# Attention and FFN block on one core: queries and keys in two float32r parts of 48 rows, batches in alternating partition halves, and a slot's exponent banks ahead of its maximum banks

## What is computed

```python
xn = layernorm(x)                                   # x: 8 batches x 512 tokens x 256
Q, K, V = xn @ W_q.T, xn @ W_k.T, xn @ W_v.T        # 16 heads of 16 values
Qr, Kr = rope(Q), rope(K)
scores = einsum('bhqd,bhkd->bhqk', Qr, Kr) * 16 ** -0.5   # causal mask
attn = softmax(scores) @ V, heads joined, @ W_o.T
ffn = fake_fp8(xn) @ fake_fp8(weight).T + bias      # one scale for each tensor
out = x + attn + ffn
```

## Time and profile before

| | |
|---|---|
| median of 3 runs | 481.37 us (481.06 to 482.79) |
| the profiled execution's span | 479.7 us |
| PE busy | 413.3 us, 86% |
| DVE busy | 352.8 us, 74% |
| ACT, POOL busy | 278.5 us, 274.8 us |
| DMA moved | 57.55 MB, mean 120 GB/s |

### The profile page before, as it was taken

One profiled execution on the slowest core, in us unless ns is written; L12 is line 12 of the kernel. 1 busy time (PEld: TensorE's weight loads), 2 busy tenths in 40 slices (PEclk: granted clock), 3 DMA queues, 4 the chain that ended last, 5 costly groups with the idle time before them and its releaser, 6 DMA issues.

```text
span 479.7 us, 10238 instructions
## 1 busy us (share of the span) xinstructions
PE 413.3 (86%) x2819; PEld 224.7 (47%) x2819; DVE 352.8 (74%) x1340; ACT 278.5 (58%) x500; POOL 274.8 (57%) x278
## 2 busy tenths in 40 slices
PE   1771667899999999999999969999999999998976
PEld 1431411264346455645564535545555544554544
DVE  3779799868779887988798827978897868852041
ACT  2734731047765776577657742587468665666840
POOL 2204576436747963796389631985498427327560
PEclk9995555599999999999999986999999999999997
DMA  7728458211482339323923391145714671020021
GB/s 249 254 76 223 107 178 198 66 46 44 153 202 93 100 104 199 135 86 117 243 92 108 109 227 48 44 135 152 189 56 135 165 196 39 5 86 6 1 87 45
DMA packets 39789, 57.55 MB, mean 120 GB/s; under 512 B 5280, under 2 KB 31264, under 8 KB 39712
## 3 DMA queue, kind: packets, MB, share of 16 engines
q1 hardware_dynamic: 39744, 57.03, 42.0%
HBM read 35.78 MB, written 17.04 MB: 110 GB/s over the span
## 4 chain that ended last, share of the span: by engine, by line
PE 44%; POOL 18%; DMA 11%; issue 11%; ACT 7%; DVE 4%; SPq 3%; ACTq 0%; POOLq 0%; DVEq 0%
PE o_ps L935 9%; PE st_ps L854 9%; DMA qk_parts<-parts 8%; PE s_ps L871 7%; PE m_ps L907 5%; PE m_ps L810 4%; POOL parts L268 4%; PE m_ps L882 4%; ACT prob L734 3%; POOL prob L440 3%; POOL rot L264 3%; POOL rot L258 2%; POOL xq L470 2%; SPq L370 2%; POOL qv L466 2%
## 5 line engine op out<-in xcount | busy, mean ns | idle before, releaser
L599 DVE CUSTOM_DVE_ANT_0 scratch<-s_ps,causal 128x512 bf16<-128x512 f32 (+3 forms) x512 | 224.2, 487 | 64.4 <-PE s_ps L871 53.7
L734 ACT ACTIVATE prob<-st_ps 128x512 f32<-128x512 f32 x320 | 175.6, 600 | 104.4 <-PE st_ps L854 104.2
L440 POOL TENSOR_SCALAR_AFFINE_SELECT prob<-prob 128x512 f32<-128x512 f32 (+1 forms) x160 | 86.8, 546 | 141.8 <-ACT prob L734 141.0
L871 PE MATMUL s_ps<-k_st,q_st 96*128 96x512 bf16 (+3 forms) x512 | 132.4, 322 | 21.8 <-DVE rowmax L599 18.6
L854 PE MATMUL st_ps<-q_st,k_st 98*128 98x128 bf16 (+3 forms) x512 | 121.1, 303 | 1.0 <-ACT prob L734 0.9
L935 PE MATMUL o_ps<-prob,v_sb 128*17 128x512 f32 (+3 forms) x1024 | 87.8, 439 | 6.0 <-ACT heads L749 5.2
L871 PEld LDWEIGHTS s_ps<-k_st,q_st 96*128 96x128 bf16 x512 | 47.1, 99 | 73.3 <-DVE rowmax L599 48.2
L854 PEld LDWEIGHTS st_ps<-q_st,k_st 98*128 98x128 bf16 x512 | 43.5, 98 | 64.5 <-ACT prob L734 26.8
L599 DVE DVE_READ_ACCUMULATOR2_ANT rowmax<- 128x1 f32 x512 | 42.3, 83 | 0.0
L935 PEld LDWEIGHTS o_ps<-prob,v_sb 128*17 128x17 f32 x1024 | 20.4, 96 | 44.1 <-issue 35.6
L907 PE MATMUL m_ps<-wo_sb,attnT 128*128 128x256 f32 x128 | 35.1, 398 | 1.0 <-ACT attnT L755 0.5
(11 more groups left out here) (96 smaller groups left out, 496.7 us busy)
## 6 DMA issues: line engine op xcount, KB each, us to landing
qk_parts<-parts SPq DMA_DIRECT2D x16, 768.0 KB, 3.8
q_st<-qk_parts SPq DMA_DIRECT2D x32, 192.0 KB, 3.6
k_st<-qk_parts SPq DMA_DIRECT2D x32, 192.0 KB, 3.7
q_st<-x_dram SPq DMA_DIRECT2D x8, 512.0 KB, 5.4
q_st<-qk_parts SPq DMA_DIRECT2D x32, 128.0 KB, 3.7
k_st<-qk_parts SPq DMA_DIRECT2D x32, 128.0 KB, 3.7
xn_v<-xnT SPq DMA_DIRECT2D x8, 512.0 KB, 3.7
x_res<-x_dram SPq DMA_DIRECT2D x8, 512.0 KB, 3.5
```

What stands on the lines that cost most here:

```text
L440: eng.affine_select(out=ap, in_=ap, compare_op=ALU.is_ge, fill=0.0, base=0, pattern=pat, channel_multiplier=-1).then_inc(masked, 1)
L599: eng.tensor_tensor_reduce(scratch[:, f % 2, col:col + w], s_ps[f % 2][:, col:col + w], causal[:, T - w:T], 1.0, NEG, ALU.add, ALU.max, ro ...
L734: eng.activation(prob[u][:, half * T:(half + 1) * T], st_ps[ST_BANK[2 * s + half]][:, :], ACT.Exp, scale=SCALE).then_inc(exp_done, 1)
L871: mm = eng.matmul(s_ps[f % 2][:, col:col + (qb + 1) * P], q_st[0:ROWS, 1 - par, h, qb * P:(qb + 1) * P], k_st[0:ROWS, 1 - par, h, 0:(qb + ...
```

## The change

Queries and keys are split into two float32r parts (`high`, then `low` straight from it; `remainder` and `middle` are gone). A head's stack has 48 rows (three products of 16), plus two shift rows. A batch of even number lies in partitions 0 to 49, one of odd number in 64 to 113 (`HALF * par`), so `q_st` and `k_st` hold two batches in two partition halves. In a slot the two exponent banks (`attend`) are issued first and the two maximum banks (`compare`) second. Stacks are read in two runs instead of three, 8 KB instead of 4 KB a row. The rotated values lie in the second part's place (`rotated_in`), so `rotate` waits for the store of the batch before (`parts_out`). The x batches get places of their own in eight other buffers (`x_of`), the first loops are unrolled, and the ones rows of `k_st` are written by two DMAs instead of a memset.

```diff
-Q_PARTS = ((0, 1), (0, 1, 2), (0,))
-K_PARTS = ((0, 1, 2), (0,), (0, 1))
-ROWS = 6 * DH
+Q_PARTS = ((0,), (0, 1))
+K_PARTS = ((0, 1), (0,))
+ROWS = 3 * DH
+HALF = P // 2
...
-    for n in range(4):
+    for n in range(NB):
         step(n, n % 2)
         between(n)
-    with eng.Fori(2, NB // 2) as i:
...
-        q_st = sb("q_st", [P, 2, H, T], BF16)
-        k_st = sb("k_st", [P, 2, H, T], BF16)
+        q_st = sb("q_st", [P, H, T], F32R)
+        k_st = sb("k_st", [P, H, T], F32R)
...
-        parts = sb("parts", [P, 2, 3, 2, T], BF16)
+        parts = sb("parts", [P, 2, 2, 2, T], F32R)
...
         def rotate(eng, n, w):
             eng.wait_ge(roped, 4 * n + 2 * w + 2)
             if not (isinstance(n, int) and n == 0):
-                eng.wait_ge(low_done, 2 * n + w)
+                eng.wait_ge(parts_out, 32 * (n - 1) + 16 * (w + 1))
...
-        def remainder(eng, n, w):
+        def low(eng, n, w):
             eng.wait_ge(rotated, 4 * n + 2 * w + 2)
             eng.wait_ge(hi_done, 2 * n + w + 1)
-            buf = rotated_in(n, w)
-            eng.tensor_tensor(buf, buf, parts[:, w, 0], ALU.subtract).then_inc(rem_done, 1)
-        def low(eng, n, w):
-            eng.wait_ge(mid_done, 2 * n + w + 1)
-            eng.tensor_tensor(parts[:, w, 2], rotated_in(n, w), parts[:, w, 1], ALU.subtract).then_inc(low_done, 1)
+            eng.tensor_tensor(parts[:, w, 1], rotated_in(w), parts[:, w, 0].bitcast(F32), ALU.subtract)\
+               .then_inc(low_done, 1)
...
                 for g in range(NG):
+                    if g == 0 and isinstance(n, int) and n == 0:
+                        eng.wait_ge(consts, 6)
+                        for first in (ROWS, HALF + ROWS):
+                            eng.dma_start(k_st[first:first + SHIFT, :, :].rearrange("p h (a t) -> p (h a) t", t=P).bitcast(F32),
+                                          ones2[:, None, :].to_broadcast([SHIFT, H * NQ, P])).then_inc(ones_in, 16)
                     read_stack(n, par, g, "k", busy)
...
-            eng.memset(k_st[ROWS:ROWS + SHIFT, :, :, :].rearrange("p a h t -> p (a h t)").bitcast(F32),
-                       float(np.array([0x3F803F80], np.uint32).view(np.float32)[0])).then_inc(consts, 1)
...
                     for half in range(2):
-                        i = 2 * s + half
+                        for at in range(2):
+                            if 3 in stages and at < len(unit_parts(u, half)):
+                                attend(s, half, at)
+                    for half in range(2):
+                        for at in range(2):
+                            if 2 in stages and at < len(MAX_BANKS[(2 * s + half) % len(MAX_BANKS)]):
+                                compare(2 * s + half, at)
+                def attend(s, half, at):
...
+                    h, lo = g * HG + j, HALF * par
+                    mm = eng.matmul(st_ps[ST_BANK[i]][:, col:col + T - kb * P],
+                                    k_st[lo:lo + ROWS + SHIFT, h, kb * P:(kb + 1) * P],
+                                    q_st[lo:lo + ROWS + SHIFT, h, kb * P:T], start=True, stop=True)
...
+                def compare(f, at):
...
+                    h, lo = 2 * pair + i, HALF * (1 - par)
+                    mm = eng.matmul(s_ps[f % 2][:, col:col + (qb + 1) * P],
+                                    q_st[lo:lo + ROWS, h, qb * P:(qb + 1) * P],
+                                    k_st[lo:lo + ROWS, h, 0:(qb + 1) * P], start=True, stop=True)
```

More of the change, by code:

```diff
@@ L244, in work, with rotated_in @@
             return [(s, kind, k) for s, kind, k in MISC if stage_of[ahead[kind][k]] in stages]
-        def rotated_in(n, w):
-            own = isinstance(n, int) and (n, w) == (0, 1)
-            return heads[:, 0:2, :] if own else rot[:, :, :]
+        def rotated_in(w):
+            return parts[:, w, 1].bitcast(F32)
         def rotate(eng, n, w):
@@ L366, in read_stack @@
                 src = qk_dram[par, w].rearrange("t r j h n -> (t r j) h n")
-                row = 0
+                row = HALF * par
                 for run_ in runs:
                     rows = DH * len(run_)
-                    eng.dma_start(dst[row:row + rows, par, h0:h0 + HG, :],
+                    eng.dma_start(dst[row:row + rows, h0:h0 + HG, :].bitcast(F32),
                                   src[DH * run_[0]:DH * run_[0] + rows, h0:h0 + HG, :]).then_inc(stack_in[g], 16)
@@ L405, in _ @@
                               base=0, pattern=[[-1, P]], channel_multiplier=1).then_inc(consts, 1)
+            eng.memset(v_sb[:, :, :, :], 1.0).then_inc(consts, 1)
             def invert(n, p):
@@ L456, in iteration @@
                         if s in (5, 10):
-                            remainder(eng, n, s // 10)
+                            low(eng, n, s // 10)
                     if 4 in stages:
@@ L693, in parts_of_first @@
                         high(0, w)
-                        middle(0, w)
                     high(1, 0)
@@ L846, in scores @@
                     g, u = divmod(s, 5)
-                    if u == 0 and g % 2 == 0:
+                    if 3 in stages and u == 0 and g % 2 == 0:
                         eng.wait_ge(shift_in[g // 2], 16 * (b + 1))
                     for half in range(2):
-                        i = 2 * s + half
-                        wait_past(eng, exp_done, HALVES * b + ST_BEFORE[i] + 1)
-                        for j, kb, col in unit_parts(u, half):
-                            h = g * HG + j
-                            mm = eng.matmul(st_ps[ST_BANK[i]][:, col:col + T - kb * P],
-                                            k_st[0:ROWS + SHIFT, par, h, kb * P:(kb + 1) * P],
-                                            q_st[0:ROWS + SHIFT, par, h, kb * P:T], start=True, stop=True)
+                        for at in range(2):
+                            if 3 in stages and at < len(unit_parts(u, half)):
+                                attend(s, half, at)
@@ L857, in scores @@
                         mm.then_inc(st_full, 1)
-                        if half == 0 and 2 in stages:
-                            scores_for_max(2 * s)
-                def scores_for_max(f):
+                def compare(f, at):
                     pair, m = divmod(f, len(MAX_BANKS))
-                    if f % (BANKS // NG) == 0:
+                    if at == 0 and f % (BANKS // NG) == 0:
                         g = f // (BANKS // NG)
-                        eng.wait_ge(stack_in[g], 16 * 6 * (n + 1))
-                    wait_past(eng, max_done, ITEMS * n + (ITEMS_UP_TO[f - 2] if f >= 2 else ITEMS_UP_TO[f - 2] - ITEMS))
-                    for i, qb, col in MAX_BANKS[m]:
-                        h = 2 * pair + i
-                        mm = eng.matmul(s_ps[f % 2][:, col:col + (qb + 1) * P],
-                                        q_st[0:ROWS, 1 - par, h, qb * P:(qb + 1) * P],
-                                        k_st[0:ROWS, 1 - par, h, 0:(qb + 1) * P], start=True, stop=True)
-                    mm.then_inc(s_full, 1)
+                        eng.wait_ge(stack_in[g], 16 * 4 * (n + 1))
+                    if at == 0:
+                        wait_past(eng, max_done,
+                                  ITEMS * n + (ITEMS_UP_TO[f - 2] if f >= 2 else ITEMS_UP_TO[f - 2] - ITEMS))
+                    i, qb, col = MAX_BANKS[m][at]
+                    h, lo = 2 * pair + i, HALF * (1 - par)
+                    mm = eng.matmul(s_ps[f % 2][:, col:col + (qb + 1) * P],
+                                    q_st[lo:lo + ROWS, h, qb * P:(qb + 1) * P],
+                                    k_st[lo:lo + ROWS, h, 0:(qb + 1) * P], start=True, stop=True)
+                    if at == len(MAX_BANKS[m]) - 1:
+                        mm.then_inc(s_full, 1)
@@ L966, in iteration @@
                 for s in range(SLOTS):
-                    if 3 in stages:
+                    if 2 in stages or 3 in stages:
                         scores(s)
-                    elif 2 in stages:
-                        scores_for_max(2 * s)
-                    if 2 in stages:
-                        scores_for_max(2 * s + 1)
-                        if 3 not in stages:
-                            spread_maxima(s)
+                    if 2 in stages and 3 not in stages:
+                        spread_maxima(s)
                     for at, item in enumerate(todo):
```

83 lines of the change are left out of this document (34 added, 49 removed).

## The result

The changed kernel takes 529.71 us (median of 4 runs, 523.49 to 552.47) against 482.08 us (median of 4, 481.06 to 482.83): the ratio is 1.0898, 95% interval 1.0833 to 1.0964. The prediction was 524 us in a range of 478 to 542. The profiled execution has a span of 524.7 us, 45.0 above that of before.

What follows compares the result with a forecast made beforehand. The prediction took PE's order of work to bound the main loop. It summed 479.7 + 19.5 + 41.5 - 18.2 - 2 + 1.9 = 522.4 us for the profiled execution, with the median 1.7 above: 524 us, range 478 to 542.

Steps and rivals of the forecast that it cites:

- the likeliest case: Main loop: shape changes cost and the halves overlap at slot seams; 492 to 538 us, 524 as summed, chance 0.52.
- What bounds it: Main loop: PE's order of work is the time, busy 46.0 of 47.2 us; gains on other engines count almost nothing.
- 1, float32r matmuls: Score matmuls in float32r cost more, mostly in 128-column banks: +2.6 us an iteration, +19.5 us in all.
- rival E: Short float32r score matmuls take the two float32 passes: 551 us, chance 0.03.
- 2, changes of shape: Between half-array scores and other items: 0.18 us a change into a bare load, 5.8 us an iteration, +41.5 us.
- 3, two halves at once: At slot seams, last exponent and first maximum matmuls overlap: 2.6 us an iteration, -18.2 us in all.
- Full iterations of 52 to 54 us: Main loop: the iteration length named beforehand as a sign that the forecast was right.
- the 0.09 us behind an item: Sign of a right forecast: a score matmul behind an item starts some 0.09 us late, its load starting with it.
- 4, what moves: Lighter POOL and ACT work, stores, stacks and DMAs cost 0; PE's own waits may shrink: -2 us in all.
- 5, the start: Before the main loop: -2.1 us from dropped remainders, +4 us in iteration -1 from bare loads; sum +1.9 us.
- the clock: Main loop: a clock below 1.00 was named as what would break all of the forecast; no size given.

Runs made afterwards that it cites:

- whole-array run: Changed kernel with score matmuls reading 98 and 96 rows of a constant float32r tile from iteration 0 on, in the whole-array shape: 520.79 us.
- bfloat16 run: Kernel before with its bfloat16 score matmuls cut to rows 0 to 49 and 0 to 47 of the same stacks: 508.53 us, ratio 1.0487.
- one-half run: Changed kernel with score matmuls reading 50 and 48 rows of a constant float32r tile from iteration 0 on, all in partitions 0 to 49: 593.28 us.
- 66-row run: Changed kernel with score matmuls reading 66 rows of a constant float32r tile from iteration 0 on, in the whole-array shape: 530.68 and 531.33 us.

## Why the prediction was right, and which steps were not

The total, the sign and the likeliest case were right: changes of shape cost, halves overlap, and PE's time is the kernel's. The size of several terms was not, and errors of both signs cancelled. That the total came so close is luck: without the half clock (an estimate of 19 us, below) and the start's wait (7.9 us), neither of which the sum had, the profiled execution would have taken some 498 us, not the 522.4 of the sum.

**What bounds it.** Right. In the changed kernel's full-clock iteration PE is busy 48.0 of 49.3 us, and nothing shows a gain from POOL's and ACT's lighter work (33.3 to 30.1 and 31.4 to 29.5 us), though no run has it alone. But "a gain on another engine counts almost nothing" no longer holds: six slots of an iteration wait for VectorE's `row_max`, an estimate of 3.9 us.

**1, float32r matmuls.** Nearly right. The forecast was 2.6 us plus 1.1 for the bare loads behind `pv` (counted in part 2), 3.7; the whole-array run measures +4.0. In that run a pair of 128 and 384 columns takes 0.06 + 0.23 = 0.29 us from start to start, against the 0.285 worked out from a transpose, so the half-rate rival E fell. The sum was right and its split was not: the next matmul was to stand 0.11 us behind the one of 128 columns, and it stands 0.06 behind it.

**2, changes of shape.** The mechanism is right, the price was a little high: 26 new ones at 0.18 us were 4.7, measured 3.8 (0.15 each). The bfloat16 run shows the drain by itself, 0.09 us, as forecast. Start by start, the one-half run has 4.3 us more than the whole-array run at and behind the changes, and two slots that wait for `row_max` give back 0.6 of it: most of the miss is a cost that fell into a wait. The rule of the Trainium skill that the prediction named ("TensorEngine Tiling (Array Packing)", Key Properties: a change of tiling mode drains the TensorE) agrees with these traces: 0.09 us a change.

**3, two halves at once.** This step failed, beyond its own bounds of 0 and -3.7 us an iteration: measured -5.8. The step read "the other three quarters of the scores follow one in their own half and can't". They did: TensorE started a maximum matmul while an exponent matmul written before it had not begun (208.73 before 209.06). The step also left out what the overlap runs into: where `row_max` has not yet freed the bank, the halves follow each other.

**Full iterations of 52 to 54 us** were named as the mark of a right forecast. They took 49.3. The forecast had 5.8 us more for such an iteration, the run 2.1. Of the other marks, the 0.09 us behind an item came; the first `compare` came 0.01 us behind the first `attend` of the slot, not the last; and the clock fell below 1.00 in the main loop, which the prediction had named as what would break all of it.

**4, what moves.** Wrong for one queue: the shift rows' DMAs were not among those costed. Stack reads at twice their time were given no cost because of 10 us of slack in the main loop; at the start there is no such slack, and what came late was the small store behind them, 7.9 us. The 2 us that PE's own waits were to give back did not come: in an iteration at full clock they are 0.8 us for ACT and 0.4 for VectorE, before 0.8 and 0.3.

**5, the start.** The first maximum matmul comes at 53.9 instead of 57.1 us, -3.1 where -2.1 was forecast; iteration -1, from there to the first exponent matmul without its wait, takes 37.6 instead of 35.0, +2.6 where +4 was. These are single traces; in the variants of the changed kernel the first maximum matmul comes between 53.4 and 56.5.

**Not in the sum at all: the clock.** It was only named as what would break the forecast. Without the start's stretch, about 54 us of the changed kernel's main loop stand at half clock, before 10, at the back edge. At the 0.43 us that one such us costs in the one-half run, that is an estimate of 19 us; at the 0.35 of the 66-row run it is 15.

Put together for the profiled executions: start to iteration 0 +6.7 us (V's projection at 100.9 instead of 94.2), seven iterations of 2.0 at full clock +14, half clock +19, from iteration 7 to the end +4.8 (58.8 against 54.0): 44.5 of the 45.0 us measured. The seven iterations are an average: the one with the back edge is 5.3 us longer than before at equal half clock, mostly by VectorE's longer stop there, and iteration 6, at full clock in both, 3.2. The forecast had 42.7 for the same: its seven full-clock iterations were 21 too dear (34.8 for 14) and iteration 7 one, while 19 of clock and 5 at the start, the wait less what the start gained, were missing.

## What to carry to other kernels

Price a change of operand layout in three separate terms, each with a run that has only that term: type, array shape, and halves side by side; here they were +4.0, +3.8 and -5.8 us of a 47.2 us iteration, which the total hides. When a matmul is cut to fewer rows, read the granted clock by stretch as well as the starts. A forecast that hits the total is not thereby confirmed: compare the marks named beforehand, iteration by iteration. And when TensorE begins to overlap work, look next at the engine that frees its banks.

## What the runs showed of the hardware that was not expected

- Matmuls of different row halves do not keep the written order: one written third began 0.01 us after the first and 0.33 us before the second. Where the banks were free, a slot's four banks took 0.72 us; where a maximum bank had to wait for `row_max`, its matmul began 0.04 us after the read's end and the slot took up to 1.89 us.
- Going between a 50-row half and the whole array cost 0.09 us in bfloat16, and 0.15 us on average with float32r scores.
- The same program fell to 1.2 GHz for 34 us, from iteration 0 on, with 66 rows, and not at all there with 98. In the 23.8 us at full clock before the fall PE was busy for 23.0; in the 98-row run's 23.9 us at the same place it was busy for 23.1, and the clock stayed.
- A 32 KB store behind 48-partition stack reads let the next DMA start after 12.7 us, ahead of them after 2.8 us.
- At a hardware loop's back edge VectorE stood still for 8.2 us in the kernel before and 12.5 in the changed one; written out, the iteration took 47.3 instead of 56.2 us.
